# First mixture of a decoder kernel: the expert stage gathers its token rows by a table built on TensorE, in place of a scatter into zeroed slots

## The reference, cut to what matters

```
logits = xf @ router_w.T
scores = softmax(logits)
topk_w, topk_idx = top_k(scores, 8)
slot_expert = topk_idx.reshape(-1)                 # token by token, 16384 entries
onehot = one_hot(slot_expert, 64)
pos = (cumsum(onehot, axis=0) * onehot).sum(-1) - 1
valid = pos < 128
dest = where(valid, slot_expert * 128 + pos, 64 * 128)
buf = zeros((64 * 128 + 1, 512)).at[dest].set(xf[slot_token])
yb = (silu(xb @ w_gate) * (xb @ w_up)) @ w_down    # per expert, 128 rows each
out[token] += yb[dest] * topk_w
```

## Time and profile before

| what | us |
|---|---|
| three runs, median (range) | 4962.67 (4956.53 to 4965.86) |
| profiled execution, span from first to last instruction | 4953.7 |
| routing stage c1, first to last DMA issue of its own | 2092.78 to 2289.41 |
| its last DVE instruction ends | 2235.67 |
| expert stage c2, first DMA issue | 2296.28 |

### The profile page before, as it was taken

How to read it: one execution, slowest core, us unless ns; L and a number is a source line. 1 busy time by engine, 2 the same in 40 slices (tenths; PEclk the granted TensorE clock), 3 DMA queues, 4 the chain that set the end, 5 groups by cost and what they waited for, 6 DMA issues and landing times. The chain is left out here.

```text
span 4953.7 us, 62201 instructions
## 1 busy us (share of the span) xinstructions
PE 3940.3 (80%) x19774; PEld 3051.4 (62%) x19774; DVE 2817.3 (57%) x4906; ACT 1646.4 (33%) x3379; POOL 1437.1 (29%) x1236
## 2 busy tenths in 40 slices
PE   7885999989999697753995994787878688828993
PEld 7885777767777475542553883555656476606772
DVE  5554444453444476871224874999999755523335
ACT  4343222232222120020222674555555422203431
POOL 0001101110000005663113542999999600020002
PEclk9998999999999798956997997999899899958996
DMA  3324566653333452144996546222222211033324
GB/s 112 122 85 152 117 132 123 131 128 86 83 102 87 129 167 69 40 166 151 334 318 211 182 135 226 77 85 81 81 81 89 80 53 63 30 110 123 105 96 121
DMA packets 557200, 602.49 MB, mean 122 GB/s; under 512 B 166070, under 2 KB 439543, under 8 KB 551425
## 3 DMA queue, kind: packets, MB, share of 16 engines
q1 hardware_dynamic: 508720, 491.05, 32.0%
q0 software_dynamic: 43520, 101.18, 8.2%
q10 hardware_dynamic: 4816, 8.53, 0.5%
HBM read 444.17 MB, written 198.34 MB: 130 GB/s over the span
## 5 line engine op out<-in xcount | busy, mean ns | idle before, releaser
L2274 PE MATMUL d_py<-d_h,d_ident 128*128 128x256 f32 x2048 | 529.6, 416 | 169.9 <-POOL d_h L2104 151.9
L2112 POOL TENSOR_TENSOR d_dBu<-d_B,d_dtu 128x1024 f32<-128x1024 f32 x256 | 597.1, 2364 | 117.9 <-DMA d_dt<-dt 117.9
L2274 PEld LDWEIGHTS d_py<-d_h,d_ident 128*128 128x128 f32 x2048 | 418.0, 208 | 277.8 <-POOL d_h L2104 180.0
L722 PE MATMUL a_pB<-a_uhi,a_whi 128*128 128x512 f32 x1152 | 495.1, 430 | 49.4 <-DVE a_ulo L609 43.5
L722 PE MATMUL a_pB<-a_uhi,a_wlo 128*128 128x512 f32 x1152 | 464.6, 403 | 0.0
L722 PE MATMUL a_pB<-a_ulo,a_whi 128*128 128x512 f32 x1152 | 463.8, 403 | 0.0
L2158 ACT ACTIVATE d_ph<-d_dt,d_A 128x255 f32<-128x255 f32 x1024 | 425.8, 461 | 0.2
L2218 DVE TENSOR_TENSOR_SCAN d_ph<-d_ph,d_dBu 128x1024 f32<-128x1024 f32 x160 | 366.0, 2287 | 24.4 <-ACT d_ph L2158 12.1
L1054 POOL TENSOR_TENSOR b_kv<-b_c 128x128 f32 (+11 forms) x256 | 100.3, 432 | 801.9 <-DMA b_c<-ctx_turned 797.3
L722 PEld LDWEIGHTS a_pB<-a_uhi,a_whi 128*128 128x128 f32 x1152 | 225.0, 195 | 117.6 <-DVE a_wlo L613 36.5
L695 DVE SCALAR_TENSOR_TENSOR a_W<-a_pG,a_cB,a_M 128x256 f32<-128x256 f32 (+1 forms) x384 | 142.7, 413 | 217.5 <-PE a_pG L743 193.7
(11 more groups left out here) (461 smaller groups left out, 9459.7 us busy)
## 6 DMA issues: line engine op xcount, KB each, us to landing
c_gu<-w_gu SPq DMA_DIRECT2D x64, 768.0 KB, 8.3
a_wraw<-w_bc SPq DMA_DIRECT2D x48, 768.0 KB, 7.4
a_alall<-alpha SPq DMA_DIRECT2D x24, 1024.0 KB, 5.0
slots<-a_idz POOLq DMA_DIRECT2D x64, 256.0 KB, 4.6
c_wd<-w_down SPq DMA_DIRECT2D x64, 256.0 KB, 7.8
c_xb<-slots SPq DMA_DIRECT2D x64, 256.0 KB, 9.2
slots_y<-c_y POOLq DMA_DIRECT2D x64, 256.0 KB, 6.9
f_w1r<-w SPq DMA_DIRECT2D x64, 256.0 KB, 2.7
```

Of the source, the lines that this page charges most:

```text
L722: ins = nc.tensor.matmul(out, a[:, k, cols], b[:, k, ts], start=(k == 0 and n == 0), stop=(k == F - 1 and n == 2))
L2112: pool.tensor_tensor(dBu[c % RB][:, :, :], B_sb[i][:, q * G:(q + 1) * G, :], dtu_sb[i][:, f, :].unsqueeze(1).to_broadcast([P, G, L]), ALU. ...
L2274: ins = nc.tensor.matmul(py[f % 2][:, 0:L], ident_sb[:, :], h_sb[c % RH][:, n, :], start=False, stop=(q == Q - 1 and n == G - 1))
```

## The change

The token rows are no longer scattered. In the routing stage, for each choice k of each tile, two matrices are made: `c_atplace`, 128 tokens by 128 places, one where the token has this place (8 compares per tile, on POOL; the last tile's on DVE), and `c_named`, 128 tokens by 64 experts, the token's number where it chose this expert (two ACT instructions per group). PE adds up their products in `c_pTab`, 128 places by 64 experts: 16 float32 matmuls a group, 128 in all, each group's behind the `positions` of the next group, the last group's at the end. DVE copies the sum to `slot_token` as whole numbers. The expert stage gathers its rows by column e of this table with an indirect DMA issued by POOL, eight ahead, from `x_tok`; SP's load of `c_xb` is gone, and PE waits for the gather on a semaphore of its own. Since every place reads a valid row, `slots` does not exist any more and is not zeroed; `rows`, of the second mixture, still is. `slot_token` lives in a space c0 around both stages, which adds one barrier behind the expert stage. The routing stage loads one more constant. The remaining instructions stay as they are.

The diff, cut to its core (the changed line numbers follow the kernel after):

```diff
@@ norm_route
-        ramp_sb = m.sb("ramp", [P, E_])
+        ramp_sb, tok_sb = m.sb("ramp", [P, CAP]), m.sb("tok", [P, TILES])
...
+        at_place = [m.sb(f"atplace{i}", [P, G, K_, CAP]) for i in range(2)]
+        named = [m.sb(f"named{i}", [P, G, K_, E_]) for i in range(2)]
...
-        pL, pP = m.ps("pL"), m.ps("pP")
+        pL, pP, pTab = m.ps("pL"), m.ps("pP"), m.ps("pTab")
...
-                             (before_sb[:, :], before), (ramp_sb[:, :], ramp.partition_broadcast(P))):
+                             (before_sb[:, :], before), (ramp_sb[:, :], ramp.partition_broadcast(P)), (tok_sb[:, :], tokens_of)):
...
+        def places_matched(eng, g, c):
+
+            for k in range(K_):
+                ins = eng.tensor_scalar(at_place[g % 2][:, c, k, :], ramp_sb[:, :], pk[:, c, k:k + 1], None, ALU.is_equal)
+            return ins
+
         @block.gpsimd
         def _(pool):
+            pool.wait_ge(s_const, 16 * CONSTS)
             for g in range(GROUPS):
-                i = g % BUF
-                pool.wait_ge(s_pl, g + 1)
-                for c in range(G):
-                    for k in range(K_):
-                        pool.indirect_dma_start(x_slots, bass.IndirectOffsetOnAxis(ap=pl[i][:, c, k:k + 1], axis=0), xt[i][:, c, :], None,
-                                                bounds_check=SLOTS - 1, oob_is_err=False).then_inc(s_sc[i], 16)
-            for i in range(BUF):
-                pool.wait_ge(s_sc[i], GROUPS // BUF * G * K_ * 16)
+                pool.wait_ge(s_pk, g + 1)
+                if g >= 2:
+                    pool.wait_ge(s_tab, g - 1)
+                for c in range(G if g < LAST else 1):
+                    places_matched(pool, g, c).then_inc(s_at, 1)
...
+            def name(g):
+                act.wait_ge(s_hot, g + 1)
+                if g >= 2:
+                    act.wait_ge(s_tab, g - 1)
+                for c in range(G):
+                    t = g * G + c
+                    nc.scalar.activation(named[g % 2][:, c, :, :], hot[:, c, :, :], ACT.Copy, scale=tok_sb[:, t:t + 1]).then_inc(s_named, 1)
...
                 if g + 1 < GROUPS:
                     features(g + 1)
+                name(g)
...
-                    dve.wait_ge(s_sc[i], g // BUF * G * K_ * 16)
...
+                if g:
+                    dve.wait_ge(s_named, g * G)
...
+                if g:
+                    dve.wait_ge(s_at, g * G)
+                nc.vector.tensor_reduce(flat(pk[:, :, :]), tmp[:, :, :, :].rearrange("p c k e -> p (c k) e"), AX.X, ALU.add).then_inc(s_pk, 1)
+                dve.wait_ge(s_pk, g + 1)
+                if g == LAST:
+                    dve.wait_ge(s_tab, g - 1)
+                    places_matched(nc.vector, g, 1).then_inc(s_at, 1)
...
                 route(g)
+            dve.wait_ge(s_tab, GROUPS)
+            nc.vector.tensor_copy(slot_token[:, :], pTab[:, 0:E_]).then_inc(s_set, 1)
...
+            def table(g):
+                pe.wait_ge(s_named, g * G + G)
+                for c in range(G):
+                    pe.wait_ge(s_at, g * G + (c + 1 if g < LAST else G))
+                    for k in range(K_):
+                        ins = nc.tensor.matmul(pTab[:, 0:E_], at_place[g % 2][:, c, k, :], named[g % 2][:, c, k, :],
+                                               start=(g == 0 and c == 0 and k == 0), stop=(g == LAST and c == G - 1 and k == K_ - 1))
+                ins.then_inc(s_tab, 1)
...
                 positions(g)
+                if g:
+                    table(g - 1)
+            table(LAST)
@@ moe0_experts
-                    sp.dma_start(xb[q][:, :], x_slots[bass.ds(e * CAP, CAP), :]).then_inc(s_in[q], 16)
...
-            with pool.Fori(0, E_ // U) as r:
-                for j in range(U):
-                    e, q = r * U + j, j % 2
-                    pool.wait_ge(s_y, e + 1)
-                    pool.dma_start(y_slots[bass.ds(e * CAP, CAP), :], y_sb[q][:, :]).then_inc(s_out[q], 16)
+
+            def rows(e):
+                pool.indirect_dma_start(xb[e % BUF][:, :], None, x_tok, bass.IndirectOffsetOnAxis(ap=slot_token[:, e:e + 1], axis=0),
+                                        bounds_check=T - 1, oob_is_err=False).then_inc(s_rows[e % BUF], 16)
+            for e in range(BUF):
+                rows(e)
+            for e in range(E_):
+                pool.wait_ge(s_y, e + 1)
+                pool.dma_start(y_slots[e * CAP:(e + 1) * CAP, :], y_sb[e % 2][:, :]).then_inc(s_out[e % 2], 16)
+                if e + BUF < E_:
+                    rows(e + BUF)
...
-                        pe.wait_ge(s_in[q], (r * (U // BUF) + s // BUF + 1) * 64)
+                        pe.wait_ge(s_in[q], (r * (U // BUF) + s // BUF + 1) * 48)
+                        pe.wait_ge(s_rows[q], (r * (U // BUF) + s // BUF + 1) * 16)
@@ decoder
-              a["a_log0"], a["l2_alpha"], a["l2_beta"], a["ema"], scratch("alpha0", 2, 16, P), scratch("norms0", 16, P), (slots, rows))
+              a["a_log0"], a["l2_alpha"], a["l2_beta"], a["ema"], scratch("alpha0", 2, 16, P), scratch("norms0", 16, P), (rows,))
...
+    with ExitStack() as routed:
+        slot_token = Space(nc, "c0", routed).sb("slot_token", [P, E_], U32)
+        first_mixture(nc, a, y_feat, z_feat, x2_tok, slot_token, places0, weights0)
+        moe0_experts(nc, x2_tok, slot_token, a["w_gu"], a["w_down"], a["ident"], slots_y)
```

More of the change, by code:

```diff
@@ L1117, with norm_route @@
 FAR = 1 << 20
-def norm_route(nc, v_sb, router, ident, before, ramp, x_tok, x_slots, places, weights):
+def norm_route(nc, v_sb, router, ident, before, ramp, tokens_of, x_tok, slot_token, places, weights):
     LN_EPS = 1e-5
@@ L1143, in norm_route @@
         S = m.sb("S", [P, E_])
-        pk, ok, pf = m.sb("pk", [P, G, K_]), m.sb("ok", [P, G, K_]), m.sb("pf", [P, G, K_])
+        pk, ok, pf, far = (m.sb(n, [P, G, K_]) for n in ("pk", "ok", "pf", "far"))
         wk = [m.sb(f"wk{i}", [P, G, K_]) for i in range(BUF)]
@@ L1152, in norm_route @@
         s_log, s_neg, s_exp, s_A, s_pos, s_pl = (m.sem(n) for n in "log neg exp A pos pl".split())
+        s_hot, s_pk, s_at, s_named, s_tab = (m.sem(n) for n in "hot pk at named tab".split())
         s_xo = [m.sem(f"xo{i}") for i in range(BUF)]
         s_out = [m.sem(f"out{i}") for i in range(BUF)]
-        s_sc = [m.sem(f"sc{i}") for i in range(BUF)]
         block = phase.enter_context(nc.Block())
-        LV, LL = 19, 3
-        CONSTS = 4
+        LV, LL = 17, 3
+        CONSTS = 5
+        LAST = GROUPS - 1
         def rows(a, g):
@@ L1342, in _, with moe0_experts @@
                 positions(g)
-def moe0_experts(nc, x_slots, w_gu, w_down, ident, y_slots):
+                if g:
+                    table(g - 1)
+            table(LAST)
+def moe0_experts(nc, x_tok, slot_token, w_gu, w_down, ident, y_slots):
     U, BUF = 8, 8
@@ L1365, in moe0_experts @@
         s_in = [m.sem(f"in{i}") for i in range(BUF)]
+        s_rows = [m.sem(f"rows{i}") for i in range(BUF)]
         s_T, s_xT, s_G, s_g, s_h, s_H, s_hT, s_Y, s_y = (m.sem(n) for n in "T xT G g h H hT Y y".split())
@@ L2929, in _, with first_mixture @@
                         output(n)
+def first_mixture(nc, a, y_feat, z_feat, x2_tok, slot_token, places, weights):
+    with ExitStack() as across:
+        x2_sb = Space(nc, "b0", across).sb("x", [P, KD, T])
+        ssm0_out(nc, a["x"], y_feat, z_feat, a["w_out0"], a["b_out0"], a["gate"], a["ident"], x2_sb)
+        long_conv(nc, x2_sb, a["ctx_turned"], a["taps"], a["skip0"], a["exchange"])
+        norm_route(nc, x2_sb, a["router0"], a["ident"], a["upper"], a["ramp"], a["tokens_of"], x2_tok, slot_token, places, weights)
 def decoder(nc, a, out):
@@ L2940, in decoder @@
     u_feat, u_tok, z_feat, y_feat = scratch("u0_feat", 12, P, T), scratch("u0_tok", T, 1536), scratch("z0_feat", 12, P, T), scratch("y0_feat", 12, P, T)
-    slots, slots_y = scratch("slots", SLOTS, D), scratch("slots_y", SLOTS, D)
+    slots_y = scratch("slots_y", SLOTS, D)
     rows, rows_y = scratch("rows", EX * SEL, D), scratch("rows_y", EX * SEL, D)
@@ L2951, in decoder @@
     x3_tok = scratch("x3_tok", T, D)
-    with ExitStack() as across:
-        x2_sb = Space(nc, "b0", across).sb("x", [P, KD, T])
-        ssm0_out(nc, a["x"], y_feat, z_feat, a["w_out0"], a["b_out0"], a["gate"], a["ident"], x2_sb)
-        long_conv(nc, x2_sb, a["ctx_turned"], a["taps"], a["skip0"], a["exchange"])
-        norm_route(nc, x2_sb, a["router0"], a["ident"], a["upper"], a["ramp"], x2_tok, slots, places0, weights0)
-    moe0_experts(nc, slots, a["w_gu"], a["w_down"], a["ident"], slots_y)
+    with ExitStack() as routed:
+        slot_token = Space(nc, "c0", routed).sb("slot_token", [P, E_], U32)
+        first_mixture(nc, a, y_feat, z_feat, x2_tok, slot_token, places0, weights0)
+        moe0_experts(nc, x2_tok, slot_token, a["w_gu"], a["w_down"], a["ident"], slots_y)
     u1, z1, dt1, dtu1 = (scratch(n, F1, P, T) for n in ("u1", "z1", "dt1", "dtu1"))
@@ L2997, in laid_out @@
     return {
```

(2 more changed lines are left out.)

11 lines of the change are left out of this document (6 added, 5 removed).

## The result

The changed kernel takes 4936.16 us (median of 4 runs, 4931.11 to 4942.95) against 4961.18 us before: a ratio of 0.9945, 95% interval [0.9931, 0.9959]. In a second set of runs it was 4934.67 against 4963.53 us, 0.9944 [0.9931, 0.9958]. It is 25 to 29 us faster; the forecast was 19, a time of 4944 us.

What follows compares the result with a forecast made beforehand. Bounds: DVE busiest in routing, an uncovered scatter tail of some 60 us (the target), PE in the expert stage. Terms -49.2 + 26.1 + 3 + 1.2 = -18.9 gave 4944 us; forecast band 4936 to 4953, whole range 4912 to 4957.

Steps and rivals of the forecast that it cites:

- Zeroing: Scan's first half: the 64 zeroing DMAs on POOL's queue were hidden whole, so dropping them gives 0 us.
- Tail: End of routing stage: last tables, compares, copy and two clears replace the uncovered scatters, -49.2 us.
- Loop: Routing cycles: DVE waits for PE's table, 4.0 us in five cycles and 6.1 in a sixth, +26.1 us.
- Expert start: Start of expert stage: eight gathers share the DMA engines with the first weights, between -1 and +7, taken as +3 us.
- Expert stage: Expert stage after its start: PE stays the bound, gathers eight experts (42 us) ahead cover their landing, 0 us.
- Constant and barrier: One more constant load ahead of PE's start (0.4) and one more barrier behind the experts (0.8), +1.2 us.
- The offset: Whole kernel: profiled span 9.0 us below the runs' median; the two kernels' difference taken as the same in both.
- The first, the clock: Routing stage: PE's clock rises to 2.4 GHz, a table takes 3.52 us, sum -50.6, 4912 us; chance 22%.
- The second, stores and gathers in one queue: Expert stage: gathers in POOL's queue delay stores, DVE then PE wait, +102 us, 5046 us; chance 8%.
- The third, POOL beside DVE: Routing stage: POOL's compares delay DVE's short instructions behind `c_pk`, 2.7 us a group, 4955 us; chance 12%.

Runs made afterwards that it cites:

- The base: The changed kernel once more, unaltered, for the follow-up runs to be compared with: 4934.67 us (5 runs), ratio 0.9944.
- the two reduced kernels: The changed kernel with one table matmul per group in place of 16, 4919 us; the same with one POOL compare of eight besides, 4911.22 us.

## Why the prediction was right

**Zeroing, 0.** Right, by the run with it put back: 2 us between the medians, inside their ranges.

**Tail, -49.2; measured -48.35.** The table's 7.04 us was exact (7.03). The two clears took 2277.03 - 2275.83 = 1.2 us and not 1.6. POOL's compare was mis-sized: 0.454 us by the earlier trace rows, and it is 0.608.

```profile
L1185 POOL TENSOR_SCALAR c_atplace<-c_ramp,c_pk 128x128 f32<-128x128 f32 x120 | 70.5, 608 | 100.5 <-DVE c_pk L1294 100.5
```

Eight are 4.8 us and not 3.6, the cover of group 6's table is used up, and 1.39 us of waiting come in its place. The prediction had named this point ("just covered").

**Loop, +26.1; measured +23.7 with the constant.** By cycles it is +0.25 for the first, which has no table, +17.5 for the five of +4.0 each, and +5.9 for the one of +6.1. The mechanism was shown by taking the matmuls away (20.9 us go), by halving them (the cycle falls by 3.2) and by moving half of them (the same 3.2). Two sizes were off. DVE waits 2.91 us and not 3.66, because it arrives 7.21 us behind the positions' start (2164.69 - 2157.48) and not 6.73, because the tokens start 9.02 us behind it and not 9.22, and because the statistics follow the tokens' start by 1.10 us and not 1.17. Of the 0.48, 0.32 are `c_pf`, `c_pl` and `c_wk`, which took 178, 174 and 175 ns on the mean before and take 243, 288 and 314 beside POOL's compares. Then the cycles before were not all 16.6: two took 17.1 and 17.6 us, and DVE's wait for scatters, 1.0 us in all there, fell away with them. The base and the two reduced kernels (159.17, 138.26, 135.41 us) do not divide the 23.7 us between table and compares: 20.9 is what comes back with the matmuls gone and the compares there, 2.85 what comes back with most compares gone besides. In the changed kernel itself DVE waits 2.91 us for PE in each of the five cycles, which covers what the compares cost it; no run took the compares away and kept the table.

**Expert start, +3; measured +2.9: the size was luck.** It was picked between -1 and +7. The lines show where it is, PE's transposes for the second expert: before, after, and with four ahead.

```profile
2308.20 1.11 PE L1446 MATMUL c_pT<-c_ident,c_xb 128*128 128x128 f32 x4 [3.03 <-DMA c_xb<-slots]
```

```profile
2291.52 1.12 PE L1492 MATMUL c_pT<-c_ident,c_xb 128*128 128x128 f32 x4 [4.88 <-DMA c_wd<-w_down]
```

```profile
2282.81 1.12 PE L1493 MATMUL c_pT<-c_ident,c_xb 128*128 128x128 f32 x4 [4.80 <-DMA c_wd<-w_down]
```

They start 11.92 us behind the stage's first DMA before and 14.49 after: 2.6 of the 2.9 us. What they wait for is now the second expert's weights, where it was the rows that SP loaded behind these. The second expert's `c_gu` takes 8.2 us to land where it took 5.9, the third's 12.9 in place of 7.4. With four gathers ahead these are 7.6 and 10.3, and PE starts at 13.46 (with five or six at 14.3). So gathers of rows wanted later do hold up the weights, as the prediction said, but four in place of eight give back only 1.0 us of the 2.6. What the rest is due to was not separated, and from the start to the first `c_y` runs of equal code in this stage differ by up to 2.1 us.

**Expert stage, 0; measured 0.0.** Right, and in part by luck: the lead was put at 42 us and is 21, against a chain of 7.5. DVE's wait for stores, 49.4 us in all before, is 48.3.

**Constant and barrier, +1.2; measured -2.7 behind the last `c_y`, where +0.8 was said.** The trace shows the place. At the end of the stage POOL drains, before and after:

```profile
L1349 POOLq DRAIN  x1: 5279/5279/5279, 2657.7 to 2657.7; - x1
```

```profile
L1388 POOLq DRAIN  x1: 2504/2504/2504, 2641.0 to 2641.0; - x1
```

That is 2.8 us less. The last store is issued 0.98 us behind the start of its copy where it was 1.34, another 0.4 us, and from the drain's end to the next stage's first DMA it is 1.15 us where it was 0.76: this is the added barrier, +0.4 and not +0.8. Why the drain is shorter is open.

**The offset.** The sum was made against a profiled span 9.0 us below the median. In the changed kernel a run's time is 1.7 us over its span (4937.38 and 4935.7); with the kernel before it is 2.8 to 3.6 us over it in the 23 executions that have both. So some 6 us of the 9 were that the profiled execution of before was a quick one, and 1.3 us of the gain in the medians lie outside the spans, which the sum had taken to be the same in both.

**Rivals.** The first, the clock: false as it was priced, with the table at 3.52 us and a cycle near the old one. Over 149 us with PE busy for 111, in runs of 16 us without a gap (2157.48 to 2173.42 above), the granted clock stayed at 0.50, the 1.2 GHz level; where other executions had 0.59 and 0.60, the tables still took 7.03 to 7.04 us and the cycle 20.03 or more. The rule of the Trainium skill, TensorE: Matmul & The Clock Gate, part 1, that sustained matmul activity releases the throttle, is not what this trace shows for such work; it is, where PE is busy for 99% (1.00 in the expert stage). The second, stores and gathers in one queue: false, by DVE's wait for stores (48.3 us, 49.4 before) and by the run with the gather first (4 us); what a short lead costs is another thing, rows that come late. The third, POOL beside DVE: true in kind, 0.3 us a group behind `c_pk`, hidden in five groups by DVE's wait, as the prediction had it; and 1.39 us in the last compares. The Trainium skill, SBUF — State Buffer, section Who interferes with whom, has DVE instructions with two SBUF inputs contend with one on POOL that reads SBUF, under an exclusive lock, so that the later one would wait for the end of a compare of 0.6 us. The traces agree that two inputs are hit, and not with the lock: `c_wk` is one of these and gains 135 ns on the mean, while `c_ok` of the line above it, with two inputs as well, stays at 174 to 175 ns. And in the cycle above `c_wk` starts at 2164.35, inside a compare of 2164.29 to 2164.89, and ends at 2164.69 before it.

## What to carry to other kernels

Work that is added to a loop in which two engines wait for each other costs by where it stands: look for the wait of the engine that gets it (here PE's 4.46 us ahead of the positions) and put there what fits, before making the work itself shorter. A prefetch that is issued behind a result in a software pipeline has the pipeline's depth taken off its lead, so count it in steps between the issue and the use; here four ahead was none and cost 350 us, and six were as good as eight. A clock that differs from one execution to the next can pass for the effect of an edit, so compare it by cycle before crediting either. Where two engines of unlike speed share the last small jobs of a stage, divide them so that both end together.

## What was not expected of the hardware

- With wide matmuls added, the clock was 0.75 in the first groups (0.61 without them) and fell back later with PE busier (54.6 of 61 us at 0.58). With the table in halves a cycle with PE busy for 15.36 of 17 us had 0.50. Executions of the same routing code differed: 0.50 to 0.60.
- In float32r a matmul with 64 columns left one record where float32 left two, and 16 took 3.60 us in place of 7.03.
- A 128x128 compare with a scalar per partition took POOL 0.60 us and DVE 0.23 (8 in 1.83 us).
- POOL issued indirect gathers of 128 rows of 2 KB in 1.0 us each, and in the expert stage this disturbed neither DVE's pace (331.4 us from first to last `c_y`, as before) nor the stores beyond 0.3 us (7.2 against 6.9 us to landing).
